# Two transformer layers on one core: layer 1's experts as three float32r products, with the split made beside layer 0's attention

## The reference

```python
xn = layernorm(x)
x = x + attention0(xn) + experts0(xn)      # softmax attention mixed with a linear memory; 8 experts, F = 176, top 2
xn = layernorm(x)
x = x + attention1(xn) + experts1(xn)

# attention1: q, k, v = silu(xn @ Wq), ...; chunks of 128 tokens, 16 heads of 16, per-head decay,
#   a running state S; the output is gated, RMS-normalised by head and multiplied by Wo
# experts1: router logits, top 2 of 8, weights from a softmax, and for every expert e
g = silu(x @ w_gate[e]) * (x @ w_up[e])    # w_gate, w_up: 256 x 512
y = g @ w_down[e]                          # 512 x 256
out = out + combine[:, e:e+1] * y
```

## Time and profile before

| | us |
|---|---|
| median of 3 runs | 1058.32 |
| lowest, highest | 1055.16, 1066.89 |
| the profiled execution | 1045.42 |
| its span in the trace | 1043.6 |
| TensorE busy, whole span | 878.9 (84%) |
| DVE, ACT, POOL busy | 572.6, 406.5, 312.0 |

### The profile page before, as it was taken

One profiled execution on the slowest core, in us unless ns is written; L12 is line 12 of the kernel. 1 busy time (PEld: TensorE's weight loads), 2 busy tenths in 40 slices (PEclk: granted clock), 3 DMA queues, 4 the chain that ended last, 5 costly groups with the idle time before them and its releaser, 6 DMA issues. The chain is left out here.

```text
span 1043.6 us, 15136 instructions
## 1 busy us (share of the span) xinstructions
PE 878.9 (84%) x4672; PEld 515.5 (49%) x4672; DVE 572.6 (55%) x1269; ACT 406.5 (39%) x686; POOL 312.0 (30%) x250
## 2 busy tenths in 40 slices
PE   3779999939989998999988857169999999999973
PEld 3755666501224444434434646146666656666652
DVE  7535788347877766678674323624433433343337
ACT  2225566605564566467547504002222222222210
POOL 2022666463001320151015003033333443333231
PEclk9989899955998987998998857569999999999985
DMA  9413455475221423333303303798634445343354
GB/s 276 113 31 122 131 186 184 160 196 139 87 68 52 112 91 122 122 102 111 132 24 110 111 21 122 206 261 259 198 92 92 102 104 119 86 86 92 71 167 146
DMA packets 158770, 130.58 MB, mean 125 GB/s; under 512 B 64288, under 2 KB 140336, under 8 KB 158704
## 3 DMA queue, kind: packets, MB, share of 16 engines
q1 hardware_dynamic: 151552, 110.18, 36.9%
q0 software_dynamic: 7152, 19.54, 6.6%
HBM read 83.67 MB, written 46.01 MB: 124 GB/s over the span
## 5 line engine op out<-in xcount | busy, mean ns | idle before, releaser
L1292 DVE TENSOR_REDUCE b_negmax<-b_psM 128x1 f32<-128x512 f32 x256 | 162.7, 682 | 66.6 <-PE b_psM L1454 64.1
L1223 ACT ACTIVATE b_probs<-b_psE 128x512 f32<-128x512 f32 x256 | 138.8, 595 | 121.6 <-PE b_psE L1472 120.8
L1454 PE MATMUL b_psM<-b_kst,b_qst 96*128 96x512 bf16 x256 | 100.6, 438 | 29.2 <-DMA b_vst<-scratch_v 13.7
L1472 PE MATMUL b_psE<-b_qst,b_kst 98*128 98x512 bf16 x256 | 90.2, 414 | 15.3 <-ACT b_probs L1223 11.0
L1818 POOL DMA_INDIRECT scratch_ys<-d_y,d_put x39 | 40.3, 1034 | 130.5 <-ACT d_y L1855 127.8
L1991 PE MATMUL d_psG<-d_w,d_xT 128*128 x156 | 76.8, 616 | 2.8 <-issue 1.9
L1481 PE MATMUL b_psV<-b_probs,b_vst 128*32 128x512 f32 x512 | 74.9, 658 | 2.9 <-ACT b_probs L1223 2.9
L1824 POOL TENSOR_TENSOR d_rs<-d_ss,d_neghalf 128x16 f32<-128x16 f32 x16 | 47.0, 2938 | 98.9 <-DVE d_ss L1920 98.9
L1999 PE MATMUL d_psU<-d_w,d_xT 128*128 x156 | 74.8, 602 | 0.0
L2016 PE MATMUL d_psY<-d_w,d_hidden 128*128 x312 | 74.8, 382 | 0.0
L1472 PEld LDWEIGHTS b_psE<-b_qst,b_kst 98*128 98x128 bf16 x256 | 20.8, 99 | 107.7 <-ACT b_probs L1223 53.7
(11 more groups left out here) (353 smaller groups left out, 1685.1 us busy)
## 6 DMA issues: line engine op xcount, KB each, us to landing
scratch_parts<-a_parts SPq DMA_DIRECT2D x12, 512.0 KB, 4.3
b_qst<-scratch_parts SPq DMA_DIRECT2D x96, 64.0 KB, 2.3
b_kst<-scratch_parts SPq DMA_DIRECT2D x96, 64.0 KB, 2.3
scratch_parts<-b_part SPq DMA_DIRECT2D x24, 256.0 KB, 3.3
d_qst<-scratch_parts SPq DMA_DIRECT2D x96, 64.0 KB
d_kst<-scratch_parts SPq DMA_DIRECT2D x96, 64.0 KB
scratch_ys<-a_y SPq DMA_DIRECT2D x39, 128.0 KB, 1.7
scratch_v<-a_xn SPq DMA_DIRECT2D x4, 1024.0 KB, 6.8
```

The lines of the kernel that those rows point to most:

```text
L1223: nc.scalar.activation(probs[k % PSLOTS][:, h, :], psE[h % 2][:, :], ACT.Exp, scale=float(HD) ** -0.5).then_inc(scores_used[h % 2], 1)
L1292: nc.vector.tensor_reduce(negmax[i][:, t, h:h + 1], psM[:, h % 2, :], AX_X, ALU.max, negate=True).then_inc(rows_used[h % 2], 1)
L1454: nc.tensor.matmul(psM[:, h % 2, :], qst[g][0:STACK, h, t * P:(t + 1) * P], kst[g][0:STACK, h, :], start=True, stop=True).then_inc(rows_re ...
L1472: nc.tensor.matmul(psE[h % 2][:, :], kst[g][0:STACKM, h, k * P:(k + 1) * P], qst[g][0:STACKM, h, :], start=True, stop=True).then_inc(score ...
```

## The change

Layer 1's expert weights are no longer read as they are. In the middle each of the 4 batches brings two experts in as 6 pieces of 128 x 1024 (gate, up and down of each). SP loads a piece in slot 0, 2, 5, 7, 10 or 13 (`SPLITS`). One slot later ACT copies it to float32r (`rawhi`), after its exponentials and its step of that slot, and POOL subtracts that from it (`rawlo`). Two slots after the load SP stores both to DRAM. Each engine does it after its step of the slot; on SP, in the last slot of a group, that is after the loads of the next batch's group. There are two buffers of each kind.

Layer 1 keeps a ring of three experts (high and low part, 3.1 MB each) in the room of `d_w`. SP loads experts 0 to 2 at the start, and each later one when the last block of the expert three before has gone through its down product; the block numbers come from the routing (`leave`). Gate, up and down are three float32r products each; xT and hT are split by ACT (copy) and DVE (subtraction). `turn` of block b + 3 now comes ahead of `down` of block b.

The q and k stacks are stored by the middle in their final order of 96 rows: 12 DMAs for each of q and k of a batch where there were 3. Of a chunk, layer 1 then loads each stack by one DMA, v, kd and sg by one (they are stored side by side), and qd by one. The first two chunks are loaded by SP, the others by ACT, behind its copy of normT. The results of the experts are read back into two buffers, so that the third and fourth wait for the first and second `combine`.

```diff
+PARTS1 = 12
+RING = 3
+SPLITS = (0, 2, 5, 7, 10, 13)
+PIECE = 1024
...
+        def piece(slot, behind):
+            return SPLITS.index(slot - behind) if slot - behind in SPLITS else None
...
+            def load_piece(b, j):
+                p = len(SPLITS) * b + j
+                if not (isinstance(p, int) and p < 2):
+                    sp.wait_ge(raw_lo, p - 1)
+                src = io[("gate1", "up1", "down1")[j % 3]][2 * b + j // 3].rearrange("(k p) n -> p k n", p=P)
+                sp.dma_start(raw[j % 2][:, :].rearrange("p (k n) -> p k n", k=HT1 if j % 3 == 2 else KT), src).then_inc(raw_in[j % 2], 16)
+
+            def store_piece(b, j):
+                sp.wait_ge(raw_lo, len(SPLITS) * b + j + 1)
+                for i, tile in enumerate((rawhi, rawlo)):
+                    at = j % 3 * PIECE
+                    sp.dma_start(scratch["w1"][2 * b + j // 3, :, i, at:at + PIECE], tile[j % 2][:, :].bitcast(F32)).then_inc(raw_stored[j % 2], 16)
+
+            def pieces(b, slot):
+                if piece(slot, 2) is not None:
+                    store_piece(b, piece(slot, 2))
+                if piece(slot, 0) is not None:
+                    load_piece(b, piece(slot, 0))
...
                 for k in range(TILES - 1):
                     beside(k)
+                    pieces(b, TILES * g + k)
                 if not last:
 
                     sp.wait_ge(probs_used, TILES * (GROUPS * b + g + 1))
                     load(b + 1, g)
                 beside(TILES - 1)
+                pieces(b, TILES * g + TILES - 1)
+
+            def store_stack(n, op, j, order):
+                for i, part in enumerate(order):
+                    if part == j:
+                        for k in range(KT):
+                            sp.dma_start(scratch["stack1"][n, op, i * HD:(i + 1) * HD, k * HH:(k + 1) * HH, :].rearrange("d h t -> h d t"),
+                                         parts[j][:, k, :]).then_inc(part_stored, 16)
...
+                nc.gpsimd.tensor_tensor(rawlo[j % 2][:, :], raw[j % 2][:, :], rawhi[j % 2][:, :].bitcast(F32), ALU.subtract).then_inc(raw_lo, 1)
...
+            def take_piece(b, j):
+                p = len(SPLITS) * b + j
+                act.wait_ge(raw_in[j % 2], 16 * (len(SPLITS) // 2 * b + j // 2) + 16)
+                if not (isinstance(p, int) and p < 2):
+                    act.wait_ge(raw_stored[j % 2], 32 * (len(SPLITS) // 2 * b + j // 2))
+                nc.scalar.activation(rawhi[j % 2][:, :], raw[j % 2][:, :], ACT.Copy).then_inc(raw_hi, 1)
...
                     beside(k)
+                    if piece(TILES * g + k, 1) is not None:
+                        take_piece(b, piece(TILES * g + k, 1))
...
-        for kind, n in (("gate", b + 1), ("turn_h", b), ("up", b + 1), ("down", b), ("turn", b + 3)):
+        for kind, n in (("gate", b + 1), ("turn_h", b), ("up", b + 1), ("turn", b + 3), ("down", b)):
...
-        w = sb("w", [P, E, WCOLS])
+        w = sb("w", [P, RING, 2 * WCOLS], F32R)
...
+            for e in range(RING, E):
+                sp.wait_ge(y_done, leave[e - RING])
+                load_weights(e)
+                weights_loaded(e)
...
             for b in range(BATCHES):
+                if b >= 2:
+                    sp.wait_ge(added, b - 1)
...
+                    if n + 2 < CHUNKS:
+                        load_chunk(act, n + 2)
...
+            def turn_h(b, _):
+                dve.wait_ge(hT_hi, b + 1)
+                nc.vector.tensor_tensor(hT[b % 2][1][:, :, :].rearrange("p k n -> p (k n)"), psH[:, :],
+                                        hT[b % 2][0][:, :, :].bitcast(F32).rearrange("p k n -> p (k n)"), ALU.subtract).then_inc(hT_lo, 1)
...
-                for k in range(HT1):
-                    mm = nc.tensor.matmul(psY[:, 0:D], hT[b % 2][:, k, :], weights(b, DOWN + k * D, D),
-                                          start=k == 0, stop=k == HT1 - 1)
-                mm.then_inc(y_ps, 1)
+                three(nc, psY[:, 0:D], [(hT[b % 2][0][:, k, :], hT[b % 2][1][:, k, :], *weights(b, DOWN + k * D, D))
+                                        for k in range(HT1)]).then_inc(y_ps, 1)
```

More of the change, by code:

```diff
@@ L215, in __init__ @@
         self.take_done, self.put_done, self.expert_done = sem("take"), sem("put"), sem("expert")
+        if ring:
+            self.turns, self.slot, self.leave = sb("turns", [P, B]), sb("slot", [P, B], I32), sb("leave", [P, E], I32)
+            self.turned = sem("turned")
     def load(self, sp, io):
@@ L307, in positions @@
         nc.vector.tensor_scalar(self.expert[:, :], self.whose[:, :], float(E - 1), None, ALU.min).then_inc(self.expert_done, 1)
+        if self.ring:
+            R = self.ring
+            nc.vector.tensor_scalar(self.leave[:, :], self.ends[:, :], 1.0, None, ALU.add).then_inc(self.expert_done, 1)
+            nc.vector.tensor_scalar(self.turns[:, :], self.whose[:, :], float(2 * R), None, ALU.is_ge).then_inc(self.turned, 1)
+            nc.vector.tensor_scalar(self.whose[:, :], self.whose[:, :], float(E - 1), None, ALU.min).then_inc(self.turned, 1)
+            dve.wait_ge(self.turned, 2)
+            nc.vector.scalar_tensor_tensor(self.turns[:, :], self.whose[:, :], float(R), self.turns[:, :], ALU.is_ge, ALU.add).then_inc(self.turned, 1)
+            dve.wait_ge(self.turned, 3)
+            nc.vector.scalar_tensor_tensor(self.slot[:, :], self.turns[:, :], float(-R), self.whose[:, :], ALU.mult, ALU.add).then_inc(self.expert_done, 1)
     def invert(self, pe):
@@ L990, in middle @@
         y0_held = sb("y0_held", [P, 1])
+        raw = [sb(f"raw{i}", [P, PIECE]) for i in range(2)]
+        rawhi, rawlo = ([sb(f"raw{n}{i}", [P, PIECE], F32R) for i in range(2)] for n in ("hi", "lo"))
         psE = [ctx.enter_context(nc.psum_tensor(f"b_psE{i}", [P, SEQ], F32)) for i in range(2)]
@@ L1740, in states_before, with load_chunk @@
             return (UPDATES - 1) * (n // NC) + max(n % NC - 1, 0)
+        def load_chunk(queue, n):
+            s, b, t = n % 2, n // NC, slice(n % NC * CH, (n % NC + 1) * CH)
+            if n >= 2:
+                queue.wait_ge(gated[s], n // 2)
+            for op, dst in enumerate((qst, kst)):
+                queue.dma_start(dst[s][:, :, :], scratch["stack1"][b, op, :, :, t]).then_inc(chunk_in[s], 16)
+            queue.dma_start(rows[s][:, :], scratch["rows1"][b, t, ROW0:ROWS1]).then_inc(chunk_in[s], 16)
+            queue.dma_start(qd[s][:, :].rearrange("p (k n) -> p k n", k=KT),
+                            scratch["qd"][b, :, :, t].rearrange("k p n -> p k n")).then_inc(chunk_in[s], 16)
         block = ctx.enter_context(nc.Block())
@@ L1866, in light @@
                                          ACT.Copy).then_inc(normT_done, 1)
[L1868 removed]
+                    if n + 2 < CHUNKS:
+                        load_chunk(act, n + 2)
+            act.sem_inc(y_done, 1)
+            walk({"light": light, "turn": turn, "gate": gate, "turn_h": turn_h, "down": down})
         @block.vector
@@ L1997, in up @@
                     pe.wait_ge(mult_done, b)
-                for k in range(KT):
-                    mm = nc.tensor.matmul(psU[:, :], xT[b % 2][:, k, :], weights(b, UP + k * H1, H1),
-                                          start=k == 0, stop=k == KT - 1)
-                mm.then_inc(up_ps, 1)
+                three(nc, psU[:, :], [(xT[b % 2][0][:, k, :], xT[b % 2][1][:, k, :], *weights(b, UP + k * H1, H1))
+                                      for k in range(KT)]).then_inc(up_ps, 1)
             def turn_h(b, _):
```

143 lines of the change are left out of this document (68 added, 75 removed).

## The result

The changed kernel takes 1247.64 us (median of 4 runs, 1242.68 to 1252.56), the kernel before 1058.76 on the same chip: a ratio of 1.181, 95% interval 1.174 to 1.188. It is slower by 189 us, where 83 were forecast; 1247.6 lies above the range. The profiled execution took 1242.68 us, its span is 1240.9 us.

A forecast was written before the change was run, and what follows sets the result against it. TensorE was taken to bound the attention stage and layer 1's block loop. Terms 73 + 14 + 3.5 + 1 + 1 - 9.5 = +83 us on 1058.3 gave 1141 us; forecast case 1098 to 1185 (0.55), range 1050 to 1190.

The forecast's parts named there:

- Shorter products: Layer 1's block loop: float32r gate, up and down products save 0.96 us a block, 37.5 us over 39 blocks.
- hT: Layer 1's loop: a second instruction between the transposes and the down product costs 0.15 us a block.
- normalising chain: Layer 1's loop: fixed-length chain from a chunk's output to its transposes, with less work covering it; 9 us lost.
- I take ... 0.5 us a chunk: Layer 1's loop: cost of four chunk loads in ACT's queue behind normT, 14 times.
- Stack stores: End of the attention stage: nine more issues for k's stack on the path, +3.5 us (bounds 1 and 7).
- Raw waits: Attention stage: ACT's copies wait for raw pieces loaded late on SP's queue, holding up exponentials; 73 us (bounds 40 and 87).
- Clock: Attention stage: nine added waits of 3.5 us or more lower TensorE's granted clock, 1.5 us each, 14 us.
- Registers: Layer 1's loop: weight addresses from registers, 24 a block for 8, and one more register load; 6 us.
- The ring: Layer 1's weight ring isn't late; rival (d), that it stalls TensorE, was among others at 0.05 in all.
- Start, read-back: Layer 1: five more DVE routing steps at the start, +1 us; read-backs waiting for the first two combines, +1 us.
- Layer 1 in all: Layer 1's loop: saves 37.5 us, gives back 28, so gains 9.5 us (bounds -37 to +20).
- Rival (c): Layer 1's loop gains nothing or loses through ACT's chunk loads and register instructions: +9.5 to +30, some 1165 us; chance 0.14.

The follow-up runs named there:

- e8: Changed kernel with SyncE issuing layer 1's later chunk loads, plus TensorE reading the next block's two registers right behind the gate products: layer 1 366.3 us, from 386.1.
- e1: Changed kernel with layer 1's loads of chunk 2 and later issued by SyncE instead of ScalarE: layer 1 386.1 us, from 439.9.
- e10: Changed kernel with raw pieces loaded earlier, three part stores each for q and k, later chunk loads on SyncE, early register reading: 1.003 of the kernel before.
- e6: Kernel before with only the final-order stacks: twelve stores each for q and k, two loads a chunk on SyncE: 1.028 of before, stage 486.6 us.
- e4: Changed kernel with q and k parts stored by three DMAs each, put together by ScalarE's chunk loads: stage 547.2 us from 588.9, layer 1 477.1 from 439.9.
- e2: Changed kernel with each raw piece loaded one piece earlier: attention stage 495.0 us, from 588.9.
- e5: Changed kernel with early raw loads, three part stores each for q and k, later chunk loads on SyncE: 1.012 of before, stage 474.9 us.
- e11: Kernel of e10 with the rounding copy on GpSimd instead of ScalarE: attention stage 475.9 us.
- e12: Kernel of e10 without the 48 stores of the halves, layer 1 taking unrounded weights: attention stage 462.5 us.

## Why the prediction was wrong

The direction and the main mechanism were right; the size was not, and the time fell above the range. By its own steps:

- **Shorter products: right**, but for the first interval of a group. Otherwise the matmuls start 0.23 and 0.12 us apart as in the earlier trace rows, and a gate product of six takes 1.39 us where nothing disturbs it. From its first start to the next instruction a gate, up and down product takes 1.45, 1.48 and 1.53 us in e8 (medians of 39 blocks) and took 1.77, 1.77 and 1.76 before: 0.84 us a block and 33 us in all, where 37.5 were forecast. Timeline of TensorE in e1, a whole gate product and the end of a down product:

```profile
905.50 0.40 PE L63 MATMUL d_psG<-d_w,d_xT 128*128 x1
905.74 0.40 PE L64 MATMUL d_psG<-d_w,d_xT 128*128 x1
...
906.66 0.39 PE L65 MATMUL d_psG<-d_w,d_xT 128*128 x1
906.89 0.60 PE L2089 MATMUL d_psH<-d_ident,d_h 128*128 128x128 f32 x4
...
912.67 0.28 PE L64 MATMUL d_psY<-d_w,d_hT 128*128 x1
912.79 0.28 PE L65 MATMUL d_psY<-d_w,d_hT 128*128 x1
```

  The Trainium skill's four passes for true FP32 (FP8 and Floating Point Precision, TensorE Precision Notes) would make three products 0.75 of one; 1.39 against 1.72 is 0.81.

- **The loop's other terms, without ScalarE's loads and the registers: right as a sum.** -37.5 + 6 (hT) + 9 (normalising chain) is -22.5; e8 and e10, which take away both of the others, show layer 1 at 366 for 386, -20. As the products gave 33 and not 37.5, the two prices together were a little smaller than forecast. The normalising chain is the one seen: TensorE's weight loads waited 15.7 us for it in e1's loop for the 7.7 of the earlier trace rows, 8 more where 9 were forecast. hT was not measured by itself.

- **"I take ... 0.5 us a chunk": the step that failed worst.** 7 us forecast, 54 measured (e1). I had priced an issue by its shortest rows, 0.45 us, "at least", four times, and then let 0.5 of these 1.8 us count; the earlier trace rows, which it names, already had six issues in 3.76 us, and the same loads on SyncE in layer 1 took 2.8 to 9.6 us for six. And I took the price as time on a queue, while ScalarE's steps for the blocks stand behind it. The Trainium skill (DMA: Bandwidth & Descriptors, Issuing engines are not separate DMA queues) calls the time to start a DMA "usually small relative to the DMA itself". I cited its first half only; the second holds for ten of the 14 loads of k's stack (0.85 to 1.04 us of issue, where in e1 this load lands 6.3 us after its issue, the median) and not for the other four, 3.48 to 8.41 us.

- **Stack stores, +3.5: failed.** 29 us by the times of e6, 42 by the stage of e4. An issue takes 0.81 us and not 0.46, and the wait behind it was missed: VectorE may not write the next parts before the last store has landed (26.1 us in four waits).

- **Raw waits, +73, with their clock, +14: mechanism right, 94 us for 87 (e2).** Of the waits, slot 8 was 12.8 for 10.5 and slot 1 in batch 2 20.4 for 11.7, both from what stands ahead in SyncE's queue.

- **Clock, +14: too small.** TensorE's busy time for the same matmuls rose by 32 us, of which e2 gives back 26. It isn't apart from the waits: e10, with 376.6 us at 0.87, has all but 3 back:

```profile
220.50:682.00 461.50, 376.58 (x1840) 176.20 (x1840) 290.38 (x586) 250.49 (x379) 150.52 (x100) 0.87 0.55 175
```

- **Registers, +6: too small**, 20 (e8). **The ring: right**, no gate product waits for a DMA. **Start, read-back**: within 2 us of what was said (e1's end is 40.6 us for 39.6).

- **Layer 1 in all:** +54 for ScalarE's loads and +20 for the registers, -20 for the rest, is the +53.7 measured; the forecast had -9.5, with 7 and 6 in the places of 54 and 20.

- **Rival (c)** named the right places, ScalarE's chunk loads and TensorE's registers, at 9.5 to 30 us over a forecast that had 13 for them; they are worth 74. I had set no upper bound for an issue from a row, only "at least", and with that and the stack stores the top of the range, 1190, was too low.

How the pieces add: the span grew by 197.3 us, 147.6 in the attention stage and 53.7 in layer 1, less 4.0 in layer 0. Taken back one at a time, late loads and stack stores give 94 and 42 of the 147.6; taken back together (e5) they give 114. So the stage keeps some 18 to 34 us for the splitting itself (470 to 475 in e5 and e10, against 441 and 452), and as two stages alike differ by up to 11 us, its size is known no better than that. Which part of it costs that stays open: neither the copies' engine (e11) nor the stores of the halves (e12) account for it alone.

## What to carry to other kernels

A DMA issue is an instruction of the engine that gives it, and its length is not a constant: before moving loads to a computing engine, read how long the very same loads held the queue they stood on, the longest rows as well, and count everything behind them on the new engine. A transfer cut into more DMAs costs twice, at the issue and at the buffer that it frees later. Where prefetched data are consumed in the next step of an in-order engine, load them one step earlier: here that was worth 94 us for an edit of a few lines.

## What the hardware showed that I had not expected

- An issue of the same DMA (k's stack, 384 KB in 1536 runs) held ScalarE for 0.90, 3.48 and 8.41 us in different chunks; the load of 512 KB of rows behind it 2.4 to 4.6 us in these, while 1 MB stored in the attention stage took SyncE 0.41 (the rows' v, at 483.45). What was under way beside it goes with the length: the four long ones (8.41 us at 833.50, 3.48 at 898.25, 4.93 at 979.43, 7.13 at 1061.10) began 1.1 to 10.6 us behind the first of two or four loads of 1.5 MB of weights on SyncE's queue (822.94, where there are four, 893.27, 975.88, 1059.96; 9.7 us to landing), and the other ten took 0.85 to 1.04 us, with no such load begun in the 9 us before. No run here takes the weights away alone, so that this is the cause isn't shown.
- In slot 8 of batch 1 SyncE's issues came 1.42 to 1.44 us apart, with durations near zero, as the rows at 396.39 to 400.69 show, while GpSimd issued its eight gathers (0.95 us each, 0.30 apart):

```profile
395.59 0.95 POOL L1235 DMA_INDIRECT b_y<-scratch_ys,b_y_at  x1 [0.30 <-issue]
396.84 0.95 POOL L1235 DMA_INDIRECT b_y<-scratch_ys,b_y_at  x1 [0.30 <-issue]
398.09 0.95 POOL L1235 DMA_INDIRECT b_y<-scratch_ys,b_y_at  x1 [0.30 <-issue]
```

  The gathers alone don't do it. In the kernel before the same eight run from 356.57 us on, and SyncE's issues of that time, v at 361.41 and the maxima at 361.97, are 0.56 us apart; in e1, with the same loads and stores in this slot, they are 0.56 to 0.64 apart (403.75 to 405.52) beside the gathers of 398.83 to 407.71, and the raw load leaves 8.0 us after the group's start (8.4 forecast, 12.8 here). What slowed them here stays open.

- The first interval of a group of float32r products is longer than the others: in e8 0.29 us on the mean of 37 gate products and 0.32 of 37 up products for 0.23, and 0.22 of 38 down products for 0.12. Over 39 blocks that is some 10 us. In the kernel before it was longer too (0.49, 0.47 and 0.24 us for 0.43, 0.43 and 0.22), some 5 us, so that the other 5 are missing from the gain.
